# A decoder layer on one core: the second narrow step of each row joins the accumulating transfers

## The reference

```python
scores = jnp.einsum('bhtd,bhsd->bhts', q, k) / SCALE
scores = jnp.where(causal[None, None], scores, NEG_INF)
attn = jax.nn.softmax(scores, axis=-1)
mask = jnp.clip((R + z[:, :, None, None] - dist) / R, 0.0, 1.0)
attn = attn * mask
attn = attn / (attn.sum(axis=-1, keepdims=True) + 1e-08)
out = jnp.einsum('bhts,bhsd->bhtd', attn, v)
```

## Time and profile before

| | |
|---|---|
| median of 3 runs | 3192.86 us (3192.83 to 3197.88) |
| the profiled execution, its own time | 3189.68 us |
| its span | 3187.9 us |
| PE busy, share of the span | 2896.6 us, 91% |
| DVE / ACT / POOL busy | 1853.1 / 1130.8 / 790.0 us |
| granted TensorE clock, mean | 0.949 |
| self-attention | about 345 to 1712 us |
| small rounds L924, records | 1792 (224 rounds) |
| accumulating transfers L703 | 96, 1 MB each, median 7.7 us to landing |

### The profile page before, as it was taken

How to read it: one execution, slowest core, us unless ns; L and a number is a source line. 1 busy time by engine, 2 the same in 40 slices (tenths; PEclk the granted TensorE clock), 3 DMA queues, 4 the chain that set the end, 5 groups by cost and what they waited for, 6 DMA issues and landing times. The chain is left out here.

```text
span 3187.9 us, 49319 instructions
## 1 busy us (share of the span) xinstructions
PE 2896.6 (91%) x18474; PEld 1645.8 (52%) x18474; DVE 1853.1 (58%) x1976; ACT 1130.8 (35%) x2670; POOL 790.0 (25%) x730
## 2 busy tenths in 40 slices
PE   7999699999999999999997899999998877777788
PEld 6877234333333334343434688888886333232345
DVE  4345498889898979888863455555554410000048
ACT  3222355555455545555552333333332101010123
POOL 0000444434344433444342122222221000000013
PEclk9999799999999999999998899999998988887889
DMA  4553767675766666666555112111212779999954
GB/s 172 182 188 132 186 140 166 136 162 135 164 143 152 154 147 143 153 148 148 124 107 182 30 63 66 66 66 66 66 66 78 275 299 421 420 420 421 420 207 161
DMA packets 215607, 555.83 MB, mean 174 GB/s; under 512 B 31534, under 2 KB 65992, under 8 KB 178585
## 3 DMA queue, kind: packets, MB, share of 16 engines
q1 hardware_dynamic: 194649, 442.24, 40.2%
q0 software_dynamic: 13824, 100.67, 16.2%
q10 hardware_dynamic: 6976, 10.75, 0.9%
HBM read 359.87 MB, written 84.14 MB: 139 GB/s over the span
## 5 line engine op out<-in xcount | busy, mean ns | idle before, releaser
L795 ACT ACTIVATE B_e<-B_pS 128x512 f32<-128x512 f32 (+3 forms) x1280 | 614.3, 533 | 611.9 <-PE B_pS L899 336.2
L749 DVE TENSOR_REDUCE mx<-B_pM 128x4 f32<-128x2048 f32 (+2 forms) x299 | 589.7, 1972 | 150.9 <-PE B_pM L885 99.5
L742 DVE SCALAR_TENSOR_TENSOR B_em_dve<-B_mask,B_e 128x1536 f32<-128x1536 f32 (+3 forms) x288 | 554.1, 1924 | 53.3 <-ACT B_e L795 47.2
L899 PE MATMUL B_pS<-B_qs,B_ks 97*128 97x512 f32 (+3 forms) x1280 | 502.4, 444 | 21.1 <-DMA B_qs<-q_hi 10.5
L695 POOL TENSOR_TENSOR B_em_pool<-B_e,B_mask 128x512 f32<-128x512 f32 (+3 forms) x288 | 385.9, 1340 | 505.3 <-ACT B_e L795 446.2
L899 PEld LDWEIGHTS B_pS<-B_qs,B_ks 97*128 97x128 f32 x1280 | 226.2, 191 | 343.2 <-issue 206.1
L933 PE MATMUL B_pD<-B_em_pool,B_ones 128*32 128x512 f32 (+3 forms) x640 | 293.4, 540 | 12.2 <-DVE B_em_dve L742 7.8
L933 PE MATMUL B_pD<-B_em_dve,B_ones 128*32 128x512 f32 (+3 forms) x1920 | 298.6, 542 | 0.0
L940 PE MATMUL B_pN<-B_em_dve,B_v 128*32 128x512 f32 (+3 forms) x1920 | 294.6, 535 | 0.0
L940 PE MATMUL B_pN<-B_em_pool,B_v 128*32 128x512 f32 (+3 forms) x640 | 290.3, 535 | 0.0
L2127 PE MATMUL E_pI<-ring,hT 128*32 128x512 f32 x1024 | 181.8, 804 | 101.4 <-DMA ring<-in_L_ffn_e_W_dram 55.2
(11 more groups left out here) (298 smaller groups left out, 5073.9 us busy)
## 6 DMA issues: line engine op xcount, KB each, us to landing
ring<-in_L_ffn_e_W_dram SPq DMA_DIRECT2D x128, 1024.0 KB, 21.9
B_e<-B_e POOLq DMA_DIRECT2D x96, 1024.0 KB, 7.7
ring<-in_L_ffn_e_Wg_dram SPq DMA_DIRECT2D x64, 1024.0 KB, 23.6
B_ks<-k_hi SPq DMA_DIRECT2D x64, 256.0 KB, 4.0
B_qs<-q_hi SPq DMA_DIRECT2D x64, 256.0 KB, 4.4
E_xq<-xT_sc ACTq DMA_DIRECT2D x18, 512.0 KB, 10.3
ring<-x_sc SPq DMA_DIRECT2D x36, 256.0 KB, 2.7
qc<-in_x_dram SPq DMA_DIRECT2D x34, 256.0 KB, 2.7
```

The source lines that it names most:

```text
L742: nc.vector.scalar_tensor_tensor(em_dve[:, f % SLOTS_DVE, :, w0:], mask_of(f, mine), 1.0, e[:, f % SLOTS_E, mine, w0:], ALU.min, ALU.mult) ...
L749: nc.vector.tensor_reduce(mx[:, :, qt, c], pM[:, :, 0:w], AX.X, ALU.max).then_inc(max_taken, 1)
L795: nc.scalar.activation(e[:, f % SLOTS_E, h, w0:], pS[:, h % SBANKS, w0:], ACT.Exp, scale=SCALE).then_inc(exp_ready, 1)
L899: last = nc.tensor.matmul(pS[:, h % SBANKS, w0:], ks[0:ROWS_S, kb // NT, h, kb % NT * P:(kb % NT + 1) * P], qs[0:ROWS_S, qb, h, w0:], star ...
```

## The change

The list of pairs takes in the diagonal step of each row, with the first narrow step (384 columns) as its partner; the change's own words count these two as the first and the second narrow step. `add_pair` then adds only the columns that the partner has, from `w0` on. POOL's loop starts its pairs one step earlier, for the pair of step 0, and has an upper bound, so that no pair is made behind the last step.

```diff
@@ -69,7 +69,7 @@
-PAIRS = [f for f, (qb, kb) in enumerate(FLAT) if kb < NT * qb and kb % 2 == 0]
+PAIRS = [f for f, (qb, kb) in enumerate(FLAT) if kb <= NT * qb and kb % 2 == 0]
@@ -700,7 +700,8 @@
                 pool.wait_ge(exp_ready, HPG * (a + 2))
-                pool.dma_start(e[:, a % SLOTS_E, :, :], e[:, (a + 1) % SLOTS_E, :, :], accum_op=ALU.add).then_inc(summed[n % 2], 16)
+                w0 = width(a + 1)
+                pool.dma_start(e[:, a % SLOTS_E, :, w0:], e[:, (a + 1) % SLOTS_E, :, w0:], accum_op=ALU.add).then_inc(summed[n % 2], 16)
@@ -710,12 +711,11 @@
-            for f in range(2):
-                weigh(f)
-            for f in range(2, ITS * STEPS + 2):
+            weigh(0)
+            for f in range(1, ITS * STEPS + 2):
                 if f < ITS * STEPS:
                     weigh(f)
-                if (f - 1) % STEPS in PAIRS:
+                if f <= ITS * STEPS and (f - 1) % STEPS in PAIRS:
                     add_pair(f - 1)
```

## The result

The changed kernel takes 3205.78 us (median of 8 runs, 3199.74 to 3209.29) against 3192.56 (8 runs) for the kernel before: ratio 1.0039, interval 1.0025 to 1.0054. In a second comparison (experiment 5) it took 3199.23 us, ratio 1.0025 (1.0015 to 1.0035). So it is slower, by 13 or 7 us, and the forecast was 28. The direction held and the time lies in the range, but the size was off by a factor of two to four. The profiled run took 3206.1 us, its span is 3204.3.

The account below looks back on a forecast made before the run. PE was taken to pace self-attention and hand its end on; first rows +36, second rows +2.4, third and fourth -10.7 gave +28 us, so 3221 us, 0.9% slower, with a range of 3183 to 3268.

Parts of the forecast that it names:

- the forecast's 0.5: Issue of a new transfer on POOL: four times the pieces add 0.5 us to the old 0.88.
- the 6.0 for pieces that cost nothing: Undisturbed landing of a new transfer if only bytes count: 7.3 - 0.25 x 5.4 = 6.0 us.
- 16 x -0.67 = -10.7: Third and fourth rows over 8 iterations: each wins the removed 384-column round, 0.67 us, with its transfer hidden.
- L = 7.9: Landing time L of the second row's new transfer, 6.6 plus 1.3 us for traffic; the row loses 0.3 us.
- The floor of 0 in the first row: First row: even a hidden transfer wins about 0, not 0.67 us, as PE waits for DVE's end.
- The rule L - 6.3: First row's change in us, with L the new transfer's time from issue to landing.
- Everything hidden: Rival: first-row landing L at most 6.3, only the floors left, -16 us, 3177 us; chance 0.17.
- The estimate of 3.8 us: Landing of a 0.79 MB transfer by the skill page's fit, 2.0 us plus bytes at 436 GB/s; source of the hidden rival.
- Pieces dear: Rival: new transfers land after 8.6 us before traffic, POOL's issue growing with the pieces; +92 us, 3285 us; chance 0.15.
- A draw: Rival: first row loses 2 us in place of 4.5, 16 us lost meet 16 won, 3193 us; chance 0.12.
- 8 x 4.5 = +36: First rows over 8 iterations: each loses 2.8 us to a landing of 9.1 and 1.7 to PE's lower clock.
- nil by itself: Each row's 512-column round moves from step a to a+2: 0.89 us less there, 0.89 more here.

Follow-up runs that it names:

- experiment 5: The changed kernel itself measured and profiled again, also called the repetition, against the kernel before: 3199.23 us, ratio 1.0025.
- experiment 1: Only the third and fourth rows of an iteration pair their diagonal step, against the kernel before: 3178.46 us, ratio 0.9955.
- experiment 2: Only the first and second rows of an iteration pair their diagonal step, against the kernel before: 3213.11 us, ratio 1.0066.
- experiment 4: The full change, with all new transfers but the very first moving all 512 columns in 128 pieces of 8192 bytes: 3229.3 us, 1.012 to the kernel before.
- experiment 7: Only the first and third rows of an iteration pair their diagonal step, against the kernel before: 3209.13 us, ratio 1.0056.
- experiment 6: Only the first and fourth rows of an iteration pair their diagonal step, against the kernel before: 3203.49 us, ratio 1.0041.
- experiment 12: The kernel before, unchanged, measured and profiled once more: 3192.92 us against 3192.44, ratio 1.0005.
- experiment 3: The full change, with the mask's near copy issued only after the first row's new transfer has landed: 3209.81 us, 1.0057 to the kernel before.
- experiment 9: The full change, with the last block's q and k loads four steps later: 3191.07 us, 1.0008 to the kernel before.

## Why the prediction was right in sign and wrong in size

**Right.** PE paces the stage, and its end is handed on (experiments 1 and 2). The undisturbed landing of the new shape, for which no row existed: 6.6 forecast, 6.7 measured, 1.32 us of issue against the 1.4 that the forecast's 0.5 amounts to. Part of that is luck: the forecast started from 7.3 us and took off 0.7, while the old shape undisturbed takes 7.0 (experiment 4) and the new one saves only 0.3; the 6.0 for pieces that cost nothing isn't seen in any row. The 0.3 us between DVE's end and the issue were read from a row whose releaser is ACT, but they hold where DVE does release (1052.22 + 1.75 = 1053.97 against 1054.28; 0.4 in third and fourth rows). Hardly a wait in third and fourth rows: 16 x -0.67 = -10.7 forecast, -14.0 measured with those two alone. The second row: L = 7.9 forecast, 7.9 measured on average, and no difference that can be measured between the kernels with and without it. The floor of 0 in the first row, set by DVE. The rule L - 6.3: in the kernel after the landing of 8.2 gives 1.9, and the row takes 2.1 us more, if one counts from PE's first sum of step 0 to that of step 4 in the timelines: 1052.18 - 1037.72 = 14.46 before, 1070.70 - 1054.12 = 16.58 after. (That count leaves out 0.3 us won just ahead of it: the round of 512 columns is gone there, and PE waits 0.53 us for DVE instead.)

The rivals. "Everything hidden" is refuted by the first rows' eight waits, 16.7 us in all. The estimate of 3.8 us by the fit of the Trainium skill (DMA: Bandwidth & Descriptors, "Anatomy of one DMA — SWDGE (gpsimd) path") isn't seen in any row: the least landing is 6.7. "Pieces dear" is refuted by experiment 4. "A draw" asked for a first row that costs 2 us in place of 4.5, "as PE's clock stays up and less traffic is left", and that describes what happened better than the forecast did. Its time of 3193 came out too low because it counted a small round won in the second row as well, where nothing is won, because the clock fell in some iterations all the same, and because the first iteration costs 5 us.

**The step that failed** is the first row's 8 x 4.5 = +36. It put 2.5 us for the full DMA engines (L = 9.1, a loss of 2.8) and 1.7 for PE's clock. Measured, over iterations 2 to 8 of the kernel after: 8.3 - 6.7 = 1.6 us of traffic, waits of 1.5 us, and a fallen clock in three of seven (none of seven in the repetition). By the four steps, less the 0.3, a first row costs 2.9 - 0.3 = 2.6 us there and 1.8 in the repetition. The first iteration costs 5.0 and 5.2 (below). So the term is 7 x 2.6 + 5.0 = +23 us, or 7 x 1.8 + 5.2 = +18, in place of +36. With the forecast's other terms, + 2.4 - 10.7, the sum is +15 or +10 us, where the medians say +13 and +7.

Why the term was mis-sized: I took the distance between loads and transfer from the timeline of the kernel before. But the change moves a round in the fourth row too, 0.86 us of PE work that slips between what releases the loads and what releases the transfer. I had booked that round's move as "nil by itself", which it is on PE. It isn't for the order of events on the queues: it gives the loads a head start, the landing and PE's wait shorten by about as much (0.8 to 1 us), and behind the shorter waits the clock mostly stayed up. Where the head start is missing (experiments 2 and 7), the forecast's row is right: 4.5 and 4.7 us by the four steps, 4.2 and 4.4 less the 0.3. In single rows it is too mild: with first and third, in the fifth iteration, 9.8 us, a wait of 3.1, half clock, and 1071.99 - 1050.94 = 21.05 us for the four steps, 6.6 more than before.

The first iteration, of which the forecast said "where the stage's first loads still run, the same is assumed": in the kernel after this holds. PE's first sum of step 7 is at 386.39 before and 391.37 after, 5.0 us later (5.2 in the repetition), but in another way: the transfer lands after 14.5 us, PE waits 5.83 for it, and a wait further on gets shorter. In experiment 2 the row's cost is paid back there: step 7's sum is at 385.85, 0.5 us earlier than before (experiments 6 and 7 lie between, 1.8 and 1.1 us later). PE's timelines, the kernel before, then the kernel after, then experiment 2's:

```profile
374.18 1.06 PE L933 MATMUL B_pD<-B_em_pool,B_ones 128*32 128x512 f32 x1 [3.46 <-POOL B_em_pool L695]
...
381.45 1.06 PE L924 MATMUL B_pD<-B_e,B_tiny 128*32 128x512 f32 x8 [1.05 <-DMA B_e<-B_e]
```

```profile
376.85 0.62 PE L933 MATMUL B_pD<-B_em_pool,B_ones 128*32 128x512 f32 x1 [1.09 <-POOL B_em_pool L695]
...
383.82 1.94 PE L924 MATMUL B_pD<-B_e,B_tiny 128*32 128x512 f32 x8 [2.87 <-DMA B_e<-B_e]
```

```profile
362.85 2.79 PE L924 MATMUL B_pD<-B_e,B_tiny 128*32 128x512 f32 x16 [5.96 <-DMA B_e<-B_e]
```

PE idles for 5.96 us in the first row of experiment 2, and the waits of 3.46 and 1.05 further on are gone. In the kernel after, the first of them is 1.09 and the second has grown to 2.87. Why the two kernels differ here isn't shown.

**What stays open.** The first two rows alone were to cost 38 us (36 + 2.4) and cost 20.6 by the medians, 24.5 by the spans of the two profiles. The rows of its profile place most of that: the stage ends 26.0 us later, with 7 x 4.2 = 29 or 30 us for the first rows of iterations 2 to 8 (forecast 31.5), -0.5 in the first iteration (forecast 4.5), -1.5 in the second rows (forecast +2.4), and some -2 in the old pairs' steps. The 3 to 5 us from there to the median lie within what two profiles of one kernel differ by.

How much of the missing 15 to 21 us is the head start's doing isn't settled. By the rows it is 7 x (4.2 - 2.6) = 11 us in the kernel after, 17 in the repetition; the times of experiments 6 and 7 say 5.6. Against that, the parts of experiments 1 and 2, which have no head start, add up to +6.6 us, no more than the whole change has. The traces show what offsets it: the first iteration costs 5.0 us in the kernel after and -0.5 in experiment 2, and PE waits 6.8 us for the second rows' sums instead of 1.9. And the old pairs' steps scatter by more than either (experiment 12). A kernel that moves the fourth row's round and changes nothing else wasn't tried.

## What to carry to other kernels

A transfer that is added to a kernel is priced by what runs on the DMA engines beside it, and that timetable has to be redrawn for the changed kernel: work that moves between two release points shifts loads against transfers, even where its own cost is nil. Where an edit applies to several places with unequal slack, price and measure each place by itself; here three of four places won 7 to 15 us, and the fourth lost more than they won. A wait behind which PE's clock falls cost about double its length here (3.1 us of wait, 6.6 us for the row, experiment 7), so a little lead for the traffic beside it can be worth more than itself.

## What the runs showed of the hardware

- An accumulating transfer of 0.79 MB in 512 pieces of 1536 bytes takes POOL 1.32 us to issue and lands after 6.7 where the DMA engines carry little else; 1 MB in 128 pieces takes 0.87 and lands after 7.0 (experiment 4). Four times the pieces cost 0.45 us on POOL, and fewer bytes pay for them.
- A head start of 0.86 us for the loads took 0.8 us off the landing (9.8 to 9.0 in the fifth iteration, 9.0 to 8.2 on average over seven, experiments 7 and 6).
- Of the loads and the mask's copy ahead of a first row's transfer, either alone left its landing at 6.8 to 6.9 us; with both it was 8.3 (means over seven iterations, experiments 3 and 9 and the kernel after).
- The length of a wait alone doesn't tell whether PE's clock falls behind it. In the kernel after the 16 products behind a wait of 1.63 us (second iteration) took 2.52 us; in experiment 2 those behind 2.54 us (sixth) took 1.50. The granted clock behind them, in the windows of the one and of the other:

```profile
542.00:546.00 4.00, 3.50 (x28) 1.46 (x32) 1.17 (x2) 0.00 (x0) 0.72 (x1) 0.60 0.58 122
```

```profile
1235.00:1239.00 4.00, 3.71 (x39) 1.61 (x39) 0.26 (x2) 0.90 (x2) 0.00 (x0) 1.00 0.46 101
```

So a forecast can give the clock a chance for such waits, but not a fixed price.
